# Making GpSimd's late scatters wait in turn for the weighted sum, in a four-layer graph network

## The reference

```python
h = relu(layernorm(x)); x = x + L0(h, ...)   # per-relation messages, averaged over the edges of a node
h = relu(layernorm(x)); x = x + L1(h, ...)   # attention: softmax over a node's edges, weighted sum of rows
h = relu(layernorm(x)); x = x + L2(h, ...)   # Chebyshev convolution: two products with the graph's matrix
h = relu(layernorm(x)); x = x + L3(h, ...)   # edge_weight * (x @ W)[src], summed by dst

# the weighted sum of L1
alpha = ex / where(denom == 0, 1, denom)[dst]
z = segment_sum(alpha[:, None] * h_src, dst, num_segments=N)
# the graph's matrix, used by L2 and L3: out[dst] += w * x[src]
```

## Time and profile before

| | |
|---|---|
| median of 3 runs | 2007.6 us (2004.83 to 2007.6) |
| the profiled execution | 2008.18 us |
| its span in the trace | 2006.4 us |
| busy: PE, DVE, ACT, POOL | 1255.5, 987.9, 199.7, 1257.9 us |
| mean granted TensorE clock | 0.713 of full |
| late scatters, first and last start | 1222.78 and 1705.21 us |

### The profile page before, as it was taken

The page is one execution under the profiler, slowest core; times in us unless marked ns, Lnnn a source line. Parts: engine busy times, 40 slices in busy tenths (PEclk is TensorE's granted clock), DMA queues, the critical chain, the costliest instruction groups (busy, mean ns, idle before and its releaser), DMA issues.

```text
span 2006.4 us, 28723 instructions
## 1 busy us (share of the span) xinstructions
PE 1255.5 (63%) x7844; PEld 1021.6 (51%) x7845; DVE 987.9 (49%) x2889; ACT 199.7 (10%) x390; POOL 1257.9 (63%) x1381
## 2 busy tenths in 40 slices
PE   5454555555563457767676664999865005599678
PEld 2354545455553456666676663999821001244323
DVE  8757565666566234344444445777540000102788
ACT  3000000000000021212111121111100000001100
POOL 0677677777778777777777777777786777000000
PEclk9778777777785655555555555999887557899799
DMA  6646455455520222222222230000236006689497
GB/s 185 206 140 187 149 161 167 149 167 170 176 56 3 58 70 78 79 77 79 76 80 79 76 80 20 1 0 0 111 151 262 0 0 262 215 347 409 173 415 310
DMA packets 154645, 272.07 MB, mean 136 GB/s; under 512 B 44030, under 2 KB 100154, under 8 KB 151546
## 3 DMA queue, kind: packets, MB, share of 16 engines
q1 hardware_dynamic: 111322, 229.57, 31.9%
q0 software_dynamic: 40064, 41.32, 8.9%
q10 hardware_dynamic: 3232, 0.82, 0.2%
HBM read 215.32 MB, written 56.29 MB: 135 GB/s over the span
## 4 chain that ended last, share of the span: by engine, by line
POOL 42%; issue 23%; PE 17%; DMA 10%; DVE 5%; ACT 1%; POOLq 1%; SPq 0%; ACTq 0%; DVEq 0%
POOL rings L735 23%; POOL pairs_by_src L752 18%; PE acc L986 7%; PE acc L1034 7%; DMA rings<-relation_rows,idx_ring 5%; DMA rings<-attention_rows,idx_ring 3%; DVE big L1825 2%; DMA pairs_by_src<-fed_val,fed_idx 1%; ACT big L900 1%; DMA big<-pairs_by_src 1%; POOL fed_val L743 1%; PE acc L992 0%; POOL fed_idx L744 0%; PE acc L1284 0%; PE acc L1224 0%
## 5 line engine op out<-in xcount | busy, mean ns | idle before, releaser
L986 PE MATMUL acc<-rings 128*65 128x128 f32 x3328 | 474.3, 307 | 256.5 <-DMA rings<-relation_rows,idx_ring 244.5
L986 PEld LDWEIGHTS acc<-rings 128*65 128x65 f32 x3328 | 414.6, 157 | 275.1 <-issue 262.5
L735 POOL DMA_INDIRECT rings<-relation_rows,idx_ring x416 | 412.7, 992 | 186.5 <-issue 124.4
L752 POOL DMA_INDIRECT pairs_by_src<-fed_val,fed_idx x416 | 423.3, 1017 | 132.6 <-issue 122.8
L1028 PE MATMUL acc<-attend_mem,rings 128*128 x1664 | 368.2, 423 | 183.5 <-DVE rings L1366 183.5
L735 POOL DMA_INDIRECT rings<-attention_rows,idx_ring x416 | 392.9, 945 | 132.2 <-issue 118.8
L1028 PEld LDWEIGHTS acc<-attend_mem,rings 128*128 128x128 f32 x1664 | 358.8, 332 | 193.1 <-issue 193.1
L1034 PE MATMUL acc<-big,attend_mem 128*64 128x512 f32 x700 | 175.3, 638 | 164.6 <-DMA big<-pairs_by_src 164.6
L1034 PEld LDWEIGHTS acc<-big,attend_mem 128*64 128x64 f32 x700 | 57.8, 146 | 260.8 <-DMA big<-pairs_by_src 175.0
L1424 DVE TENSOR_SCALAR rings<-iota_bf,col_local,score 128x256 f32<-128x256 bf16 x416 | 140.6, 409 | 44.5 <-PE acc L986 43.0
L1679 DVE TENSOR_TENSOR rings<-acc,rings 128x512 f32<-128x512 f32 x52 | 36.0, 692 | 248.7 <-DMA rings<-attention_rows,idx_ring 248.7
(11 more groups left out here) (279 smaller groups left out, 916.8 us busy)
## 6 DMA issues: line engine op xcount, KB each, us to landing
big<-pairs_by_src SPq DMA_DIRECT2D x54, 2048.0 KB, 13.5
pairs_by_src<-zeros SPq DMA_DIRECT2D x24, 1792.0 KB
big<-key_rows SPq DMA_DIRECT2D x52, 512.0 KB
rings<-local_rows SPq DMA_DIRECT2D x52, 256.0 KB, 3.3
big<-pairs_by_src SPq DMA_DIRECT2D x12, 1024.0 KB, 12.1
rings<-relation_rows,idx_ring POOLq DMA_INDIRECT x416
pairs_by_src<-fed_val,fed_idx POOLq DMA_INDIRECT x416
rings<-attention_rows,idx_ring POOLq DMA_INDIRECT x416, 2.5
```

The source lines that it names most:

```text
L735: pool.indirect_dma_start(ring[h][:, u, 0:width], None, table, bass.IndirectOffsetOnAxis(ap=idx_ring[h][:, u:u + 1], axis=0),).then_inc(ga ...
L752: pool.indirect_dma_start(pairs_by_src, bass.IndirectOffsetOnAxis(ap=fed_idx[:, h, u:u + 1], axis=0), fed_val[:, h, u:u + 1], None).then_i ...
L986: m = pe.matmul(node_sums[:, bass.ds(at[u] * P + w * P, P)], rows[h][:, u, :], onehot[h][:, u, w * P:(w + 1) * P], start=False, stop=False ...
```

## The change

Ahead of each of the scatter steps 5 to 17 GpSimd waits until `slot_free["agg"]` has reached it*4 + 2 - 16: 6 for step 5, 10 for step 6, and so on to 54 for step 17. Step 18 waits for FREED, which is 54 as well. Steps 4 and 19 to 25 have no new wait. For this the one loop over steps 5 to 24 becomes a loop over 5 to 17, step 18 as straight code, and a loop over 19 to 24. The early scatters stay as they are.

```diff
+    PACE = 4
...
-            def scatter_step(it, first=False, last=False):
+            def scatter_step(it, first=False, last=False, summed=None):
 
                 for h in range(2):
+                    if h == 0 and summed is not None:
+                        pool.wait_ge(slot_free["agg"], summed)
                     pool.wait_ge(fed, it * 4 + 2 * h + 2)
...
-            def scatter(first, end):
+            def scatter(first, end, pace=False):
 
                 a, b = first // (2 * FED), end // (2 * FED)
                 if a:
                     pool.wait_ge(scattered[0], a * (16 * FED))
                 feed(a, 0)
                 scatter_step(a, first=a == 0)
-                with pool.Fori(a + 1, b - 1) as it:
+                paced = a + 1 + (2 * IT) // PACE if pace else a + 1
+                if pace:
+                    with pool.Fori(a + 1, paced) as it:
+                        scatter_step(it, summed=it * PACE + 2 - a * PACE)
+                    scatter_step(paced, summed=FREED)
+                    paced += 1
+                with pool.Fori(paced, b - 1) as it:
                     scatter_step(it)
                 scatter_step(b - 1, last=True)
...
-            scatter(EARLY, T)
+            scatter(EARLY, T, pace=True)
```

## The result

The changed kernel takes 2028.6 us (median of 4 runs, 2025.6 to 2034.2) against 2007.3 us before (2004.8 to 2007.6): a ratio of 1.0118, 95% interval 1.009 to 1.0146. The forecast was 2032.0, in a range of 2026 to 2038. The profiled execution took 2034.22 us, with a span of 2032.4, 26.0 us more than that of before.

What follows compares the result with a forecast made beforehand. GpSimd's late scatters were taken to set the kernel's end. Wait 23.9 + resuming 0.5 + nothing given back 0 + new code 0 = 24.4 us, so 2032.0 us from 2007.6, in a range of 2026 to 2038.

Steps and rivals of the forecast that it cites:

- What bounds the kernel: GpSimd's late scatters: their end sets the kernel's end without slack, so the later gates move by the full 24.4 us.
- (a): Ahead of step 5: GpSimd waits 23.9 us for the sum's fourth half step, plus 0.5 us to resume.
- the term of 24.4: Step 5's delay in us, 23.9 waiting plus 0.5 resuming, passed in full to the kernel's end.
- stalls that fall better: Scatter stalls behind the sum may meet DVE's work differently: 4 us allowed either way, taken as 0.
- The second wait: Ahead of step 6: its release at 1283.65 comes 7.5 us early, so only the first of fourteen waits binds.
- What is given back: Beside and behind the sum: TensorE gains nothing from a quiet GpSimd and the stalls stay; taken as 0.
- (b): Unrolled step 18, second loop and open waits: taken at 0, bounded by 4 us for waits and 11.9 for passages.
- the 5.26 us gap: Before the scatter at 1687.20, one scatter behind the loop's exit: transfer count or code passage, not told apart.
- Rival 5: The sum's pace falls below GpSimd's, 6.7 us a half step; every wait binds, 79 us more: 2111 us, chance 0.03.

Runs made afterwards that it cites:

- B: Comparison against the kernel before (2008.2 us): the whole change again 1.0109, all new waits open 0.9989, only the constant wait ahead of step 5 1.0119.
- A: Comparison against the kernel before (2517.6 us): the change 0.9658, all new waits open 0.9994, only step 5's wait 1.0021, each wait four half steps fewer 0.9645.
- D: Comparison on another chip against the kernel before (2535.0 us): the change with each wait four half steps fewer 0.9613, eight fewer 0.9677.

## Why the prediction was right, and where it wasn't

**What bounds the kernel.** Right. The scatters' end set the gates, and delays of step 5 by 25, 81 and 190 us came out as 21, 81 and 186 us in the medians. In the profile of after the gates opened 2.8, 2.8 and 2.2 us later than forecast: step 5 was 0.85 us later than forecast, and the stalls behind the sum cost more, as told below.

**(a) The wait.** Forecast: release at 1269.67, 0.5 us to resume, 24.4 late. In the profile of after: 1270.36, 0.69 and 25.24, since this sum started 0.7 us later. The medians moved by 21.3 us here, 21.9 in B and 23.9 with the one wait alone. The length of the wait is the distance from step 4's last scatter to the sum's fourth half step, and that isn't fixed. From the first late scatter to step 5 it took 47.84 us in after, 44.60 in the change's run in B (1225.17 to 1269.77) and 46.32 in that of the one wait (1217.31 to 1263.63). Without a wait it took 23.03 us before and 21.19 with open waits in B, so step 4 itself varies by 2 us. Against 23.03 the wait added 24.8, 21.6 and 23.3 us. From the first late scatter to the end of the span the three took 22 to 27 us more than the two without a wait. So no run shows the term of 24.4 to be mis-sized, and both intervals of the ratio, 18 to 29 us here and 17 to 27 in B, hold it. Where the forecast's 3 us above the measured time come from stays open, since the profile is of the longest of the four executions. The range allowed for a time below the forecast by stalls that fall better; in that profile they fell worse. Ahead of all that the change touches, the start of the first late scatter alone varied from 1217.0 to 1225.2 us between executions in B, more than the miss.

**The second wait doesn't bind.** Right, by 7.6 us where 7.5 was forecast, but only as long as TensorE keeps 3.49 us for a half step.

**What is given back.** Nothing, right. The sum's pace didn't change even with GpSimd idle throughout. The stalls behind the sum stayed, 13.2 us in after against 10.8 before by the groups of eight over 10.38 (beside DVE's operations at other scatters, as in the rows here), within the 4 us allowed. The Trainium skill's page "SBUF — State Buffer", section "Who interferes with whom", has TensorE wait for no other engine's port, and lets a two-port tensor_scalar and GpSimd exclude each other; the trace agrees for L1497 behind the sum, where a scatter takes 3.23 us, and not for the one-hots. In which mode either ran the trace doesn't tell, and whether the slow issue of A and D has to do with a port no run shows.

```profile
1460.09 2.52 POOL L755 DMA_INDIRECT pairs_by_src<-fed_val,fed_idx  x1 [0.16 <-POOL fed_idx L745]
...
1474.14 3.23 POOL L755 DMA_INDIRECT pairs_by_src<-fed_val,fed_idx  x1 [0.30 <-issue]
```

and, from the timeline of VectorE:

```profile
1473.50 3.75 DVE L1497 TENSOR_SCALAR stage_mem<-rings,ext_node_f 128x3200 bf16<-128x3200 f32 x2
```

**(b) The new code.** Taken at 0 and measured as 0 (0.9989). The 5.26 us gap that I could not tell from a passage out of a loop is settled: in after step 18 is straight code and shows 5.92, as step 18 did inside the loop with 5.96. Count and load on the DMA engines explain it, and the passage adds nothing. The Trainium skill's "Runtime: NRT & Kernel Launch", section "Instruction fetch mechanics", has a taken branch to code outside the two pages held wait for a fetch; whether the branches of these loops leave the two pages no run shows, and they had no visible price.

**Rival 5 was mispriced, and it is the step that failed.** I let the sum's pace fall, had every wait bind, and took 79 us of loss. The pace did fall in A and D, and in A every wait but the last did bind, and the change gained 3.4%. The error is that I compared the slow sum under the change with the fast sum before. Where the sum is slow because of the scatters, the kernel before is bound by the sum, and a wait that hands time to it is no loss. I gave no chance to a slowing of TensorE by scatters because the trace of before shows none. That was right for the executions measured against the forecast, and it says nothing of the others.

## What to carry to other kernels

Here a wait in front of the engine whose last instruction gates the end cost its full length, whatever the pace written into it; look for the first wait that binds, and compare the periods of both sides (here 20.96 and 13.98 us) to see that the others don't. If such a wait is wanted as a safeguard for times when the other side falls behind, let it lag until it doesn't bind in the normal case (that this then costs nothing is argued here, not measured): where the sum was slow, eight half steps fewer still gave 3.2%, against 3.9% with four fewer. Before trusting one trace on what contends with what, look at comparisons taken at another time, and price a rival for both kernels under the same condition.

## What the runs showed of the hardware that I had not expected

- In two of four comparisons TensorE issued the sum's matmuls slowly while GpSimd issued scatters: 2.1 to 2.8 us apart with open waits (48 records in 100 us, where the 1529 in 166.6 us of the earlier trace rows make 918), 0.7 to 2.1 us apart between the changed kernel's pauses. It came back to its full pace within 2 to 5 us when GpSimd waited. Beside gathers it was slowed as well, but less. One and the same chip showed this in A and not in B. The time of the kernel before rose from 2008 to 2518 us by it. What causes it stays open: nothing in the profile ends these idle times, and no run here separates issuing on GpSimd from the traffic that it makes.
- GpSimd pauses ahead of the 114th and then of every 112th further indirect transfer, and the count starts anew with each stretch: in the kernel before, the 114th, 226th and 338th gather of the first layer (idle 4.72, 1.98 and 3.38 us), the same of the attention's gathers (2.06, 2.10 and 2.17), and the same of the late scatters (1.69, 5.96 and 5.26). Among the scatters it is 1.7 us with idle DMA engines and 5 to 6 us beside loads that fill them, and the same gap grew from 1.69 to 5.54 us when it was moved beside loads.
